# Decoder block with two mixtures of experts: in the mixture of 16, GpSimd rounds the weights of the second, fourth and fifth routed experts at other places of its queue

## The reference

```python
x = x + L0_attn(ln(x))     # causal, 16 heads
x = x + L0_xattn(ln(x), ctx)
x = x + L0_ffn(ln(x))      # mixture of 16 experts + 2 shared
x = x + L1_attn(ln(x))     # causal, grouped heads, rotary
x = x + L1_xattn(ln(x), ctx)   # linear attention
x = x + L1_ffn(ln(x))      # mixture of 8 experts, top 2, + 1 shared
```

```python
scores = sigmoid(hs @ gate_weight.T)         # 16 per token
# best 2 of 4 groups, then the best 6 experts in them
topk_weight = scores[topk] / sum * 2.5
for e in range(16):
    g, u = hs @ gate_proj[e].T, hs @ up_proj[e].T      # 512 -> 352 each
    out += comb[:, e] * ((silu(g) * u) @ down_proj[e].T)
y = out + (silu(hs @ shared_gate.T) * (hs @ shared_up.T)) @ shared_down.T   # inner width 704
```

## Time and profile before

| | |
|---|---|
| runs | 1959.1, 1957.86, 1953.69 us |
| the profiled execution | 1941.73 us, its span 1940.3 us |
| TensorE (PE) busy | 1805.5 us, 93% |
| VectorE (DVE) | 1111.9 us, 57% |
| GpSimd (POOL) | 1009.6 us, 52% |
| ScalarE (ACT) | 806.8 us, 42% |
| granted TensorE clock, mean | 0.97 |

### The profile page before, as it was taken

The page is one execution under the profiler, slowest core; times in us unless marked ns, Lnnn a source line. Parts: engine busy times, 40 slices in busy tenths (PEclk is TensorE's granted clock), DMA queues, the critical chain, the costliest instruction groups (busy, mean ns, idle before and its releaser), DMA issues. The chain is left out here.

```text
span 1940.3 us, 30576 instructions
## 1 busy us (share of the span) xinstructions
PE 1805.5 (93%) x10047; PEld 1564.1 (81%) x10053; DVE 1111.9 (57%) x2769; ACT 806.8 (42%) x2063; POOL 1009.6 (52%) x965
## 2 busy tenths in 40 slices
PE   6999989999699999999779999999999999998996
PEld 4888857788699999899658888888888888866796
DVE  5676785673233333335766666666666756565445
ACT  3767643222122222221256656566565433553232
POOL 3444342387773957995456546456453203115783
PEclk7999989999899999999899999999999999999999
DMA  3556430246543645554343234233331210011666
GB/s 108 161 165 202 142 136 2 75 154 226 198 168 121 214 160 179 177 174 120 88 109 103 66 94 106 63 88 97 80 75 55 73 41 9 23 49 60 218 218 196
DMA packets 104550, 232.52 MB, mean 120 GB/s; under 512 B 20672, under 2 KB 20928, under 8 KB 101328
## 3 DMA queue, kind: packets, MB, share of 16 engines
q1 hardware_dynamic: 84080, 144.31, 24.8%
q0 software_dynamic: 19744, 85.47, 13.6%
q10 hardware_dynamic: 576, 0.79, 0.1%
HBM read 126.23 MB, written 57.93 MB: 95 GB/s over the span
## 5 line engine op out<-in xcount | busy, mean ns | idle before, releaser
L706 POOL TENSOR_SCALAR a_E<-a_E,a_inv 128x128 f32<-128x128 f32 (+3 forms) x384 | 220.0, 592 | 226.9 <-DVE a_inv L842 226.9
L153 PE MATMUL bank<-f_UH,f_XH 128*128 x596 | 201.2, 338 | 23.0 <-POOL f_UL L165 18.0
L739 ACT ACTIVATE a_E<-a_E,a_top 128x512 f32<-128x512 f32 (+3 forms) x384 | 211.1, 567 | 6.7 <-DVE a_top L836 6.6
L153 PE MATMUL bank<-f_UH,f_XL 128*128 x596 | 193.4, 324 | 0.0
L153 PE MATMUL bank<-f_UL,f_XH 128*128 x596 | 193.3, 324 | 0.0
L731 ACT ACTIVATE a_PHL<-bank 128x512 fp32r<-128x512 f32 (+1 forms) x288 | 130.7, 528 | 133.4 <-PE bank L1016 133.4
L836 DVE CUSTOM_DVE_ANT_0 a_E<-a_causal,bank 128x512 f32<-128x512 bf16 (+3 forms) x384 | 163.8, 482 | 30.3 <-PE bank L1000 18.5
L153 PE MATMUL bank<-a_PHL,a_VH 128*128 128x512 f32 (+3 forms) x768 | 180.8, 324 | 0.3 <-DVE a_QL L165 0.3
L1827 DVE TENSOR_TENSOR f_gate<-bank,f_gate 128x352 f32<-128x352 f32 x79 | 41.4, 524 | 207.5 <-PE bank L153 207.4
L165 DVE TENSOR_TENSOR a_PHL<-bank,a_PHL 128x512 fp32r<-128x512 f32 (+1 forms) x288 | 153.8, 588 | 11.2 <-ACT a_PHL L731 11.1
L1772 ACT ACTIVATE f_HH<-bank 128x256 fp32r<-128x256 f32 x220 | 59.9, 324 | 234.4 <-PE bank L2169 234.3
(11 more groups left out here) (407 smaller groups left out, 4869.8 us busy)
## 6 DMA issues: line engine op xcount, KB each, us to landing
f_uraw<-f_up POOLq DMA_DIRECT2D x18, 1408.0 KB, 6.7
f_xb<-table SPq DMA_DIRECT2D x86, 256.0 KB, 3.4
table<-f_ob SPq DMA_DIRECT2D x86, 256.0 KB, 2.8
table<-a_zeros SPq DMA_DIRECT2D x31, 512.0 KB, 4.5
f_draw<-f_down POOLq DMA_DIRECT2D x27, 512.0 KB, 4.5
a_g<-a_f SPq DMA_DIRECT2D x160, 64.0 KB, 2.0
a_raw<-a_qkv SPq DMA_DIRECT2D x36, 256.0 KB
f_uraw<-f_up POOLq DMA_DIRECT2D x9, 704.0 KB, 4.5
```

The lines of the kernel that those rows point to most:

```text
L153: m = pe.matmul(out, a, b, start=first and i == 0 and j == 0, stop=last and i == n - 1 and j == 2, skip_group_check=not check)
L706: e.tensor_scalar(self.E[sl][:, a], self.E[sl][:, a], self.inv[:, sl, i:i + 1], 0.0, ALU.mult, ALU.add).then_inc(*self.s_nrm.up(N, m - 1, i))
L739: x = e.activation(E, E, ACT.Exp, scale=-1.0, bias=self.top[:, sl, i:i + 1], accum_out=self.total[:, sl, i:i + 1])
```

## The change

In the first mixture (`top` = 6) `_down(2)` moves from before choice 0 to after the scatters of choice 1. The wait for the `ends`, the register load and `_up(4)`, `_down(4)` move to after the scatters of choice 4; `_up(5)` moves to after the scatters of choice 5 and so ahead of the landing wait of choice 5; `_down(5)` follows that wait. Two helpers, `_freed_up` and `_freed_down`, hold what the loop body held. In the second mixture (`top` = 2) the instructions and their order stay as they were.

```diff
-        for w in (1, 2):
-            self._up(w)
-            self._down(w)
+        self._up(1)
+        self._down(1)
+        self._up(2)
+        if self.top < 4:
+            self._down(2)
         for j in range(self.top):
             e.wait_ge(*self.s_idx.after(N, j))
...
+            if j == 1 and self.top > 3:
+                self._down(2)
             if j == 2 and self.top > 3:
                 e.wait_ge(*self.multiplied().after(N, NT - 1))
                 self._up(3)
             if j == 3 and self.top > 3:
                 e.wait_ge(*self.s_out.after(N, NT - 1))
                 self._down(3)
+            if j == 4:
+                e.wait_ge(*self.s_ends.after(N))
+                self._freed_up(4)
+                self._freed_down(4)
+            if j == 5:
+                self._freed_up(5)
         self._all_landed(self.top - 1)
         if self.top < 4:
...
-        e.wait_ge(*self.s_ends.after(N))
-        for w in range(4, W + 1):
-            if (w - 4) % 4 == 0:
-                n = min(4, W + 1 - w)
-                regs = self.k.pool_registers[0:n]
-                self._load_bounded(e, self.k.pool_loaded[0:n], regs, self.ends[0:1, w - 4:w - 4 + n])
-            reg = regs[(w - 4) % 4]
-            if w < W:
-                e.wait_ge(self.multiplied().sem, reg)
-                e.sem_inc(*self.s_passed.up(N, "used", w))
-                self._up(w)
-            e.wait_ge(self.s_out.sem, reg)
-            e.sem_inc(*self.s_passed.up(N, w))
-            if w < W:
-                self._down(w)
+            e.wait_ge(*self.s_ends.after(N))
+            self._freed_up(4)
+            self._freed_down(4)
+            self._freed_up(5)
+        self._freed_down(5)
+        for w in range(6, W):
+            self._freed_up(w)
+            self._freed_down(w)
+        self._freed_down(W)
...
+    def _freed_register(self, w):
+        e, W, i = self.k.pool, len(self.experts), (w - 4) % 4
+        if i == 0:
+            n = min(4, W + 1 - w)
+            self._load_bounded(e, self.k.pool_loaded[0:n], self.k.pool_registers[0:n], self.ends[0:1, w - 4:w - 4 + n])
+        return self.k.pool_registers[i]
+
+    def _freed_up(self, w):
+        e, N = self.k.pool, self.name
+        e.wait_ge(self.multiplied().sem, self._freed_register(w))
+        e.sem_inc(*self.s_passed.up(N, "used", w))
+        self._up(w)
+
+    def _freed_down(self, w):
+        e, N = self.k.pool, self.name
+        reg = self._freed_register(w) if w == len(self.experts) else self.k.pool_registers[(w - 4) % 4]
+        e.wait_ge(self.s_out.sem, reg)
+        e.sem_inc(*self.s_passed.up(N, w))
+        if w < len(self.experts):
+            self._down(w)
```

## The result

The changed kernel took 1962.34 us (median of 22 runs), the kernel before beside it 1954.62 (22 runs): a ratio of 1.0029, interval 1.0016 to 1.0043. Forecast was 1941.2.

What follows compares the result with a forecast made beforehand. TensorE was taken to be held by GpSimd's queue order, in a stall worth 16.66 us (14.96 waiting, 1.70 slow clock). Taken off the timed median of 1957.86, with other steps charged nothing, this gave 1941.2 us, range 1936 to 1948.

Steps and rivals of the forecast that it cites:

- the sum: Whole kernel: 16.66 us off the profiled 1941.73 gives 1925.1; the same off the timed median 1957.86 gives 1941.2.
- the stall: First mixture, 506.8 to 521.8: TensorE waits for w = 4's low part; costs 16.66 us, 14.96 waiting and 1.70 slow clock.
- the second wait: TensorE's later wait on `f_UL`, 3.02 us at 794.24: moves with TensorE to near 777.6 and stays 3.0 us.
- What bounds the kernel: TensorE, busy 93% of the span, has one large wait on GpSimd, for `f_UL`; the order of GpSimd's queue costs the time.
- Starts and lengths of GpSimd's blocks: First mixture: up-half 10.11 us, down-half 7.28, eight scatters 9.93; first scatter at 419.1, cast of w = 4 at 497.0.
- The margin at w = 4: Low part of w = 4 ready at 505.7 to 505.9, wanted at 506.4: in time by 0.5 to 0.7 us.
- w = 7's release: GpSimd idles for w = 7 until TensorE releases w = 4's buffer, at 574.34 before; this comes 16.7 us earlier.
- The size of the gain: First mixture: the whole 16.66 us of the stall goes; full gain was given a chance of 0.78.
- the slower rival: GpSimd's moved rounding blocks VectorE's tile steps, 26.5 us of instructions at its widest, giving 1967.7 us; chance 0.03.
- No gain: Rival: stall filled but as much lost further on, or the edit fails because w = 1's wait ends late; 1957.9, chance 0.06.

Runs made afterwards that it cites:

- e1: The kernel before, unchanged, for a second profile: 1957.22 us, 0.9978 of before.
- e4: Changed kernel with w = 4 and 5 rounded behind the last landing again, so only the `_down(2)` move is left: 1961.94 us, 1.0001 of before.
- e7: Kernel before, each first-mixture scatter cut to 64 of 512 columns and sent to a tensor of its own: one run of 1966.44 us.
- e12: The kernel before, unchanged, in a sitting without late starts: 1941.41 us, 0.999 of before.
- e2: The changed kernel, unchanged, for a second profile: 1960.39 us, 0.9988 of before.
- e13: The changed kernel, unchanged, in a sitting without late starts: 1926.87 us, 0.9912 of before.
- e5: Kernel before with 7 of the 8 scatters of each choice left out in the first mixture: 1950.78 us, 0.996 of before.
- e8: Changed kernel with the rounding cut into pieces between the scatters, choice 1 left a whole run: 1952.34 us, 0.9957 of before.
- e9: Kernel before, each of the 48 first-mixture scatters replaced by a plain store and two fills on GpSimd: 1946.53 us, 1.0014 of before.
- e14: The kernel of e9 again, in another sitting without late starts: 1945.84 us, 1.001 of before.
- e16: The kernel of e9 once more, in a third sitting without late starts: 1946.48 us, 1.0012 of before.
- sitting D: Runs on chip 5 without late starts, the kernels before and after among them; kernel before at a median of 1944.20 us (21 runs).
- padded pairs: Kernels before and after, 48 scatters each replaced by a plain store and two fills, in three sittings: 12.9, 12.1 and 12.7 us apart.
- e18: The kernel of e3 in a sitting without late starts: 1926.32 us, 0.9906 of before.
- e6: Kernel before, each first-mixture scatter replaced by a plain GpSimd store of the same 256 KB: one run of 1951.88 us.
- e3: Changed kernel with `_down(2)` ahead of choice 0 again, w = 4 and 5 still moved: 1955.44 us, 0.9968 of before.

## Why the prediction was wrong

**The step that failed** stands in the sum: "The three timed runs have a median of 1957.86, 16.1 above the profiled one; I take the same 16.66 off". It carries the stall of the profiled execution over to the timed runs, and no trace from a sitting like theirs has one to take away. In the trace TensorE comes to the tenth tile at 503.80 and then stands 15 us. In e1, the same kernel at 1961.4, it comes there at 520.20, 16.4 us later, and stands for nothing: late starts have taken the stall's place. The kernels of e4 and e7 round w = 4 behind the last landing too, and their traces have no wait for it either. The two are not added to each other; the later one counts, and taking away the other gives almost nothing. The stretch from the first tile's transposes to the end of the second wait shows it (us, from each trace):

| trace | late starts marked, 430 to 530 | wait for w = 4 | first tile to second wait | from there to the end |
|---|---|---|---|---|
| before, the profile | none | 14.96 | 349.6 | 1146.1 |
| e12, before | none | 11.22 | 346.1 | 1152.5 |
| e1, before | yes | none | 346.5 | 1167.4 |
| after; e2, the same | yes | none | 343.8; 344.1 | 1169.9; 1169.9 |
| e13, after | none | none | 332.9 | 1148.2 |
| e5, one scatter in eight | none | none | 332.9 | 1173.6 |
| e8, after, paced | none | none | 334.7 | 1166.2 |

The stretch takes 346 to 350 us with the stall, 344 to 347 with late starts alone, and 333 to 335 only where both are away. Of the 16.66 us the change gives 2.8 there (e1 against after).

The last column says where the other number of that sentence belongs, the 16.1 us between profile and median. The e1 trace and the profile of before are level at the second wait (793.99 and 794.24) and 21.1 us apart at the end. 9.2 of these come up to the first `a_E` transpose (169.7 against 160.5 us), where e1 has late starts at the gathers, and 12.1 behind it; there e1 has late starts from 1820 to 1833 and from 1936 to 1939, and how much of the 12.1 is theirs is not shown. So the 16.1 us do lie outside the stretch, as the sum had it. What fails is that an execution so much longer was taken for the same in the stretch: the profiled one lies in the range of sittings without late starts, the timed runs in that of sittings with them, and there the stall is filled. The number that could have been doubted was in the text: a profiled execution 12 us below the fastest of three timed runs.

Its other steps, point by point:

- *What bounds the kernel.* Right for executions like the profiled one: the wait is there again with 11.2 us (e12) and, padded, with 9.0 to 9.7 us (e9, e14, e16).
- *Starts and lengths of GpSimd's blocks.* In e13 right within 0.4 us up to the cast of w = 4, which comes at 495.73, 1.3 early: the 0.97 us between the landing signal and the cast did not come back there.
- *The margin at w = 4*, 0.5 to 0.7 us forecast: in e13 the low part is ready at 498.36 + 6.24 = 504.60 and the up-products start on it at 506.22, 1.6 us later.
- *w = 7's release* at about 557.7: 557.32 in e13, 571.32 after.
- *The second wait stays*, with 3.0 us at 777.6: 3.00 at 777.19 in e13.
- *The size of the gain*, 16.66: 17.3 us against all runs of before in sitting D, 14.5 against those of e12, 15.2 between the two spans. That this is so near 16.66 is partly luck. The stall is smaller there (19.85 - 6.69 = 13.2 us in e12, where GpSimd comes to the cast of w = 4 at 506.53 and not at 512.87), the stretch gains 13.1 (346.1 to 332.9) and the padded pairs 10.5 to 12.4; the rest lies outside it and differs as much between traces of one kernel. The forecast of the profiled execution was 1925.1; e13's took 1926.9 and e18's 1928.69 (their medians are 1926.87 and 1926.32).
- *GpSimd's rounding beside VectorE*, the slower rival: not seen. In e13 VectorE is busy 1114.0 us, in e12 1113.6, in the profile of before 1111.9. What this rival asks for at its widest, steps of VectorE with two operands from SBUF, isn't there: in a tile they take one operand from a bank (`f_XL<-bank,f_XH`, `f_gate<-bank,f_gate`). So the runs do not test that part of the rule that the prediction cites for it.
- *No gain*, at 0.06, is the rival whose time came true, and not by its mechanism: "the stall is filled but as much is lost further on". The stall was filled before the change was made, and from upstream. No rival had the profiled execution itself as the exception.

The late starts as cause of the covered stall rest on this: e1's tile is late by 16 us and all its longer steps lie at late starts; take away the runs of indirect transfers (e5, e6) or break them (e8), and the tiles are in step in the same sort of sitting. What wasn't shown is the padded pair in a sitting with late starts, where it should gain its 12 us too; e5, e6 and e8 leave no stall to see, since GpSimd is through sooner there or has another order. Nor is it shown what about a chip or a sitting brings them on.

## What to carry to other kernels

Before a stall is priced, put the profiled execution beside the timed runs: where it lies outside their range, ask what the others do that it doesn't, and price the edit in both. A stall's worth is the distance to the next late thing on the same path, and this can come from upstream. When times agree or differ, compare the stretch that was edited and what lies behind it each by itself: a median can come out right for other reasons. In some sittings a run of back-to-back indirect transfers on GpSimd cost the other engines their starts, and laying work that GpSimd had to do anyway between them took about 9 us out of the stretch (343.8 to 334.7). Landing waits between the last gathers, which are on the path, cost 8 (28.1 against 20.3).

## What was not expected of the hardware

- In some sittings ScalarE, VectorE and, at the cast of w = 4 in three traces, GpSimd begin 1 to 5 us after their input is there, in the second half of a run of eight indirect transfers of GpSimd and up to about 1.5 us after it, often within 0.1 us of each other. Not every run has them. The kernels before and after and that of e3 have none of this in other sittings. The kernel before is 0.5 to 0.8% slower in sittings with late starts (1954.6 to 1960.6 against 1944.2 to 1944.4).
- The traces of the two sorts can be told apart before any time is looked at. In the list of DMA issues (KB each, median us to landing) the nine traces with late starts have no landing time for the tile loads, the eleven others have. Whether the one has to do with the other is not shown. First the changed kernel of the result, then e13:

```profile
f_xb<-table SPq DMA_DIRECT2D x86, 256.0 KB
```
```profile
f_xb<-table SPq DMA_DIRECT2D x86, 256.0 KB, 3.6
```

- In sittings without late starts plain stores and fills in place of the scatters bring nothing (1.0014, 1.001 and 1.0012 of before, e9, e14 and e16): there no cost of the indirect form beyond GpSimd's own time is seen.
